# Rows of group means moved to the begin of the 1x1 stage, and SyncE's transfers there in another order

## The chip, the cores and the metric

The kernel runs on one core of one Trainium2 chip. The metric is the device time in microseconds (us) of one execution; lower is better. A core has five engines that work side by side, each through its own list of instructions, and that meet only at semaphores: TensorE (PE; its weight loads are shown as PEld), VectorE (DVE), ScalarE (ACT), GpSimd (POOL), and SyncE (SP), which here only issues DMA transfers.

## The reference, cut to what matters

```
x:   (32, 512, 48, 48) float32
# layer 0, h = group_norm(x, 32 groups)
f    = relu(Wc h + bc)                      # 1x1 convolution, 512 -> 128 channels
dynW = relu(f(mean of h, maxima of h))      # a 3x3 kernel for each image and channel pair
y    = conv3x3(f, dynW) + b_ad              # 128 -> 128 channels
x1   = x + Wf y + bf                        # 1x1 convolution, 128 -> 512 channels
# layer 1
out  = x1 + grouped conv3x3(group_norm(x1), kernels)   # 32 groups of 16 channels
```

## The kernel before, in words

The loop runs over the 32 images (n). The 512 channels are four chunks of 128 (Q = 4), the rows of an image five tiles (10, 10, 10, 10 and 8 rows of 48). TensorE works through four stages for an image, and each product is three matmuls (high by high, high by low, low by high; lines 853 to 855) on halves of a value that ScalarE and VectorE make:

- A, the first 1x1 convolution (`a_tile`): one bias matmul (line 862) and four chunks of three matmuls for each of five tiles. For each tile and chunk (i = 0 to 19) ScalarE makes the high half (`x_high`, line 442) and VectorE the low half (`x_low`, line 734), in a ring of five. So i = 0 to 4 can be made before the stage begins; they are, at the end of the image before (`X_LOW_AT`). After a tile ScalarE and VectorE take its result out of PSUM (`f_high`, `f_low`; line 743).
- B, the 3x3 convolution with the image's own kernels (`b_tile`): 27 matmuls for each of five tiles, with results taken out by `y_high` and `y_low` (line 751). Beside it VectorE takes moments and maxima (lines 604 and 612) of chunks 1, 2 and 3 of the next image.
- D and C interleaved: 16 pairs (r) of grouped convolutions of layer 1 for the image before (`d_pair`), and after pairs 0, 4, 8 and 11 the six units of one chunk of the second 1x1 convolution of this image (`c_unit`). VectorE adds the residuals (`output`, line 774; `residual`, line 764).

Layer 1 needs rows above and below the image: there the padding must be the group mean, so that it becomes zero once normalized. x1 goes to a scratch tensor in HBM (`write_x1`), and so do rows of means: VectorE writes `mrow`, 128 partitions x 4 chunks x 48 (`x1_group_means`, line 682), and SyncE sends it to the scratch tensor twice (`write_means`, lines 300 and 301). Then `load_t` (lines 319 to 321) brings x1 of image n-1 back, chunk by chunk, as bands of eight rows. `load_t` of chunk 0 waits for the landing of both transfers of means, and for the store of the last chunk of image n-2 out of the same slot (`stored`); chunks 1 and 2 follow on slots of their own.

The order of the work around the change is written out by hand. VectorE's list in `step(n)` is: for tiles 1 to 4 four (at tile 1, three) `x_low` and one `f_low`, a last `f_low`, then `x1_group_means(n-1)`, which begins with the rows of means, then `x1_variances(n-1)`, then B's work. The group means themselves are made by TensorE at the end of the step before (`x1_group_means` of TensorE, line 931, behind pair 15). SyncE's list in `step(n)` is: load chunk 1 of x for image n+1 (line 288), store the last chunk of image n-2 (line 326, which waits for VectorE's `output` of pair 15), load chunks 2 and 3 of x, write the means, load tiles 0, 1 and 2 of x1 of image n-1, then `write_x1(n, 0)` in the D and C stage. All of them go through one hardware queue.

Of the kernel before, what the change touches and what calls it, by code (L numbers as in the profile page):

```python
# [13 lines left out]
N, C, H, W = 32, 512, 48, 48  # L14
Q = C // P
# [66 lines left out]
def x_slot(c, odd):  # L82

    return c if c < 1 else c + 3 * odd


def partition_of(p):

    return GC * {0: 6, 7: 7}.get(p, p - 1)
# [7 lines left out]
def build(nc, x, wct, bc, kks_in, wrow_in, b_ad, wft, bf, kt, out):  # L97
# [7 lines left out]
    with ExitStack() as ctx:  # L105
# [142 lines left out]
        def t_slot(c):  # L248
            return tb[:, T_SLOT[c], :, :, :]
# [14 lines left out]
        def reached(eng, semaphore, value):  # L264

            if not isinstance(value, int) or value > 0:
                eng.wait_ge(semaphore, value)

        def images(eng, step):

            step(0, 0, d=False)
            step(1, 1)
            with nc.Fori(2, N - 2, 2, engines=[eng.engine], hint_back_edge=True) as n:
                step(n, 0)
                step(n + 1, 1)
            step(N - 2, 0)
            step(N - 1, 1, more=False)
# [4 lines left out]
        @block.sync  # L282
        def _(sp):
            def load_x(n, odd, c):

                if isinstance(n, int) and n == 1 and c in STATS_IN_B:
                    sp.wait_ge(max_done, Q)
                sp.dma_start(xb[:, x_slot(c, odd), :], x_d[n, c]).then_inc(x_in[c], 16)

            def write_x1(n, c):  # L290

                dst, made = sc_w[n, c, :, :, AT:AT + BW], n * CUNITS + (c + 1) * OR_
                sp.wait_ge(x1_done, made)
                sp.dma_start(dst, x1b[:, c % X1_SLOTS]).then_inc(x1_out[c], 16)

            def write_means(n):

                behind, ahead = sc_m[n, 0, :, :, AT + BW:AT + BW + W], sc_m[n, OR_ - 1, :, :, AT - W:AT]
                sp.wait_ge(mrow_done, n + 1)
                sp.dma_start(behind, mrow[:, :, :]).then_inc(behind_out, 16)  # L300
                sp.dma_start(ahead, mrow[:, :, :]).then_inc(ahead_out, 16)

            def load_t(n, c):

                written = (n + 1) * 16
                above, below = partition_of(0), partition_of(IR - 1)
                dst = t_slot(c).rearrange("p j b w -> p j (b w)")
                whole = sc_k[n, c, :, :, AT:AT + BW]
                over = sc_k[n, c, M6 - GC:M6, :, AT - W:AT - W + BW]
                under = sc_k[n, c, 0:GC, :, AT + W:AT + W + BW]  # L310
                sp.wait_ge(x1_out[c], written)
                if c == 0:
                    sp.wait_ge(behind_out, written)
                    sp.wait_ge(ahead_out, written)
                if T_SLOT[c] in T_SLOT[:c]:
                    sp.wait_ge(stored[T_SLOT.index(T_SLOT[c])], written)
                else:
                    sp.wait_ge(stored[Q - 1 if c == 0 else c], written)
                sp.dma_start(dst[0:M6], whole).then_inc(t_in[c], 16)
                sp.dma_start(dst[above:above + GC], over).then_inc(t_in[c], 16)  # L320
                sp.dma_start(dst[below:below + GC], under).then_inc(t_in[c], 16)

            def store(n, c):
                dst, made = out[n, c], n * PAIRS + (c + 1) * PER_CHUNK
                sp.wait_ge(out_done, made)
                sp.dma_start(dst, t_slot(c)[0:M6].rearrange("p j b w -> p (j b w)")).then_inc(stored[c], 16)

            def step(n, odd, d=True, more=True):
                if more:
                    load_x(n + 1, 1 - odd, 1)  # L330
                if not isinstance(n, int) or n >= 2:
                    store(n - 2, Q - 1)
                if more:
                    load_x(n + 1, 1 - odd, 2)
                    load_x(n + 1, 1 - odd, 3)
                if d:
                    if isinstance(n, int) and n == 1:
                        sp.wait_ge(k_lo, K_PARTS)
                    write_means(n - 1)
                    for c in range(Q - 1):  # L340
                        load_t(n - 1, c)
                write_x1(n, 0)
                if more:
                    load_x(n + 1, 1 - odd, 0)
                if d:
                    store(n - 1, 0)
                write_x1(n, 1)
                if d:
                    load_t(n - 1, Q - 1)
                    store(n - 1, 1)  # L350
                write_x1(n, 2)
                if d:
                    store(n - 1, 2)
                write_x1(n, 3)

            for c in range(Q):
                sp.dma_start(xb[:, x_slot(c, 0), :], x_d[0, c]).then_inc(x_in[c], 16)
            sp.wait_ge(vec_const, 1)
            for dst, src in ((wc[:, :, :], wct), (wf_once, wft), (wrow[0:GATES + 1, :], wrow_in), (kks[0:GATES, :], kks_in),
                             (gates[32:33, :], bc.rearrange("(a p) -> a p", a=1)),  # L360
                             (badc[:, :], b_ad.rearrange("(p a) -> p a", a=1)), (bfc[:, :], bf),
                             (bc_rows[0:1, 0, :], bc.rearrange("(a p) -> a p", a=1)),
                             (bc_rows[32:33, 0, :], bc.rearrange("(a p) -> a p", a=1)), (kt_once, kt_flat)):
                sp.dma_start(dst, src).then_inc(const_in, 16)

            sp.wait_ge(bands_zero, 1)
            for p in range(IR):
                lo, hi = max(0, p - 2), min(OR_ - 1, p)
                k, at = partition_of(p), 2 - p + lo
                sp.dma_start(stage[k:k + GC, :, lo * GC:(hi + 1) * GC],  # L370
                             kt[:, :, at * GC:(at + hi - lo + 1) * GC]).then_inc(kt_in, 16)
            images(sp, step)
            store(N - 2, Q - 1)
            write_means(N - 1)
            for c in range(Q - 1):
                load_t(N - 1, c)
            store(N - 1, 0)
            load_t(N - 1, Q - 1)
            for c in range(1, Q):
                store(N - 1, c)  # L380
            for c in range(Q):
                sp.wait_ge(stored[c], (N + 1 if c else N) * 16)
# [158 lines left out]
        def _(vec):  # L541
# [132 lines left out]
                vec.wait_ge(dve_stat, STAT_LINKS * n + 1)  # L674
                vec.tensor_scalar(nmean[:, :], vb[:, 0, :], -1.0 / PX, None, ALU.mult).then_inc(nmean_done, 1)

            def x1_group_means(n):

                vec.wait_ge(stat_mm2, 2 * n + 1)
                reached(vec, behind_out, n * 16)  # L680
                reached(vec, ahead_out, n * 16)
                vec.tensor_scalar(mrow[:, :, :], ps[:, 32:32 + Q].unsqueeze(2).to_broadcast([P, Q, W]), -1.0, None,
                                  ALU.mult).then_inc(mrow_done, 1)
                vec.tensor_tensor(vb[:, 1, :], ps[:, 32:32 + Q], nmean[:, :], ALU.subtract).then_inc(dve_stat, 1)
                vec.wait_ge(dve_stat, STAT_LINKS * n + 2)
                vec.tensor_tensor(vb[:, 2, :], vb[:, 1, :], vb[:, 1, :], ALU.mult).then_inc(dve_stat, 1)

                vec.wait_ge(cen_done, (n + 1) * Q)
                vec.tensor_tensor(vb[:, 3, :], cen[:, :], nmean[:, :], ALU.subtract).then_inc(dve_stat, 1)
                vec.wait_ge(dve_stat, STAT_LINKS * n + 4)  # L690
                vec.tensor_tensor(vb[:, 3, :], vb[:, 3, :], vb[:, 3, :], ALU.mult).then_inc(dve_stat, 1)
                vec.wait_ge(dve_stat, STAT_LINKS * n + 5)
                vec.tensor_tensor(vb[:, 2, :], vb[:, 2, :], vb[:, 3, :], ALU.subtract).then_inc(dve_stat, 1)
# [81 lines left out]
                                         op0=ALU.mult, op1=ALU.add).then_inc(out_done, 1)  # L775

            def step(n, odd, d=True, more=True):
                for t in range(NT):
                    for i in range(t * Q, (t + 1) * Q):
                        if i >= AHEAD:  # L780
                            x_low(n, odd, i)
                    if t:
                        f_low(n, t - 1)
                f_low(n, NT - 1)
                if d:
                    x1_group_means(n - 1)
                    x1_variances(n - 1)
# [9 lines left out]
                for r in range(PAIRS):  # L797
# [5 lines left out]
                    if more and r in MOMENTS_AT:  # L803
                        c, part = MOMENTS_AT[r]
# [33 lines left out]
                x_low(0, 0, i)  # L838
            dyn_low(0)
            images(vec, step)  # L840
            x1_group_means(N - 1)
            x1_variances(N - 1)
            for i in range(SCALE_STEPS):
# [183 lines left out]
```

## Time and profile before

| | us |
|---|---|
| median of 3 runs | 3616.2 (3615.72 to 3616.76) |
| the profiled execution | 3616.31 |
| span of the profiled execution, first to last instruction | 3614.6 |
| TensorE busy | 3498.8 (97%) |
| VectorE busy | 2532.3 (70%) |
| ScalarE busy | 2109.9 (58%) |
| GpSimd busy | 965.3 (27%) |
| mean granted TensorE clock | 0.992 |

The profile has a page (totals, the span in 40 slices, the chain of work that ended last, the costliest groups) and answers on a stretch of time: instructions in order of time, busy times of windows, who waited for whom, and DMA issues with the time from issue to landing. Times are from the span's start. A busy time of an engine is that of its instructions, and instructions of an engine overlap at their ends, so start-to-start distances tell more than durations.

### The profile page before, as it was taken

How to read it: one execution, taken by the hardware profiler on the slowest of the kernel's cores; microseconds unless marked ns; L12 is line 12 of the kernel's file. 1: busy time of each engine (PE TensorE's matmuls, PEld its weight loads, DVE VectorE, ACT ScalarE, POOL GpSimd, SP SyncE). 2: the span in 40 equal slices, each digit the busy share in tenths (PEclk: the TensorE clock that was granted, in tenths of full speed). 3: DMA queues.
4: the chain of work that ended last, by engine and by line, in shares of the span. 5: the costliest groups of instructions: out<-in, count | busy, mean ns of one | idle time of the engine just before them, and what ended most of it. 6: DMA issues, size and time to landing. Idle time of an engine off the chain costs nothing.

```text
span 3614.6 us, 60228 instructions
## 1 busy us (share of the span) xinstructions
PE 3498.8 (97%) x18688; PEld 2789.1 (77%) x18688; DVE 2532.3 (70%) x5365; ACT 2109.9 (58%) x3559; POOL 965.3 (27%) x1039
## 2 busy tenths in 40 slices
PE   5799999999999999999999999999999999999996
PEld 4677877777877778877778777778777778777785
DVE  7676777776767677777667777767777777776742
ACT  4365555665555665655655556655556655556654
POOL 2033222232222232222332222322222322223323
PEclk9899999999999999999999999999999999999998
DMA  5467767677767667767677667677676777676666
GB/s 122 142 193 190 190 178 185 200 195 192 185 180 195 191 184 193 190 183 197 189 188 190 186 178 207 197 190 186 178 191 194 188 195 186 182 199 187 170 156 158
DMA packets 317577, 666.88 MB, mean 184 GB/s; under 512 B 58863, under 2 KB 288242, under 8 KB 288645
## 3 DMA queue, kind: packets, MB, share of 16 engines
q1 hardware_dynamic: 317317, 663.34, 68.5%
q8 instruction: 172, 2.82, 0.3%
q14 instruction: 88, 0.72, 0.1%
HBM read 355.00 MB, written 308.28 MB: 184 GB/s over the span
## 4 chain that ended last, share of the span: by engine, by line
PE 90%; issue 5%; DVE 4%; DMA 1%; POOL 0%; DVEq 0%; ACT 0%; SPq 0%; POOLq 0%; ACTq 0%
PE pb L853 15%; PE pb L855 15%; PE pb L854 15%; PE pac L853 7%; PE pd L853 7%; PE pd L855 7%; PE pd L854 7%; PE pac L854 6%; PE pac L855 6%; PE pac L925 2%; PE pac L862 1%; DVE x1b L764 1%; PE ps L918 1%; DMA big<-x 0%; DVE va L596 0%
## 5 line engine op out<-in xcount | busy, mean ns | idle before, releaser
L407 POOL TENSOR_TENSOR hl<-un,hl 128x384 f16<-128x384 f32 x1024 | 937.6, 916 | 2570.2 <-ACT hl L432 2566.6
L432 ACT ACTIVATE hl<-un 128x384 f16<-128x384 f32 x1024 | 539.0, 526 | 427.8 <-PE pb L855 361.7
L428 ACT ACTIVATE un<-big,b_t,s_t 128x384 f32<-128x384 f32 x1024 | 709.7, 693 | 16.1 <-DMA big<-x_rows 16.1
L853 PE MATMUL pb<-fh,dynh 128*128 128x480 f32 (+1 forms) x1440 | 548.2, 381 | 0.0
L855 PE MATMUL pb<-fh,dynl 128*128 128x480 f32 (+1 forms) x1440 | 545.3, 379 | 0.0
L854 PE MATMUL pb<-fl,dynh 128*128 128x480 f32 (+1 forms) x1440 | 544.4, 378 | 0.0
L774 DVE SCALAR_TENSOR_TENSOR big<-pd,kout,big 96x768 f32<-96x768 f32 x256 | 258.8, 1011 | 382.6 <-PE pd L855 382.6
L853 PE MATMUL pd<-hl,k_h 128*96 128x384 f16 x1536 | 507.0, 330 | 18.8 <-POOL hl L407 18.8
L774 DVE SCALAR_TENSOR_TENSOR big<-pb,kout,big 96x768 f32<-96x768 f32 x256 | 258.9, 1011 | 351.8 <-PE pb L855 351.8
L853 PE MATMUL pb<-hl,k_h 128*96 128x384 f16 x1536 | 504.9, 329 | 0.0
L854 PE MATMUL pd<-hl,k_h 128*96 128x384 f16 x1536 | 504.8, 329 | 0.0
L855 PE MATMUL pd<-hl,k_l 128*96 128x384 f16 x1536 | 504.7, 329 | 0.0
L855 PE MATMUL pb<-hl,k_l 128*96 128x384 f16 x1536 | 504.0, 328 | 0.0
L854 PE MATMUL pb<-hl,k_h 128*96 128x384 f16 x1536 | 503.9, 328 | 0.0
L454 ACT ACTIVATE xs<-pb,badc 128x480 fp32r<-128x480 f32 (+1 forms) x160 | 103.3, 645 | 670.6 <-PE pb L855 670.6
L442 ACT ACTIVATE xs<-big,negm 128x480 fp32r<-128x480 f32 (+1 forms) x640 | 397.6, 671 | 80.9 <-PE pac L855 79.7
L734 DVE SCALAR_TENSOR_TENSOR xs<-big,negm,xs 128x480 fp32r<-128x480 f32 (+1 forms) x640 | 436.3, 733 | 9.5 <-ACT xs L442 9.4
L764 DVE SCALAR_TENSOR_TENSOR x1b<-pac,bfc,big 128x384 f32<-128x384 f32 x768 | 422.4, 607 | 6.2 <-PE pac L855 5.9
L604 DVE BATCH_NORM_STATS2 bst<-big 128x6 f32<-128x384 f32 x768 | 367.2, 543 | 9.4 <-DMA big<-x 9.3
L612 DVE TENSOR_REDUCE mx<-big 128x3 f32<-128x768 f32 x384 | 339.9, 939 | 0.0
L853 PE MATMUL pac<-xs,wfh 128*128 128x384 f32 x768 | 295.7, 385 | 35.5 <-DVE x1b L764 29.3
L855 PEld LDWEIGHTS pb<-fh,dynl 128*128 128x128 f32 x1440 | 270.8, 188 | 44.0
(115 smaller groups left out, 5241.6 us busy)
## 6 DMA issues: line engine op xcount, KB each, us to landing
big<-x SPq DMA_DIRECT2D x128, 1152.0 KB, 9.8
x_rows<-x1b SPq DMA_DIRECT2D x128, 1152.0 KB, 5.6
big<-x_rows SPq DMA_DIRECT2D x128, 1152.0 KB, 12.7
out<-big SPq DMA_DIRECT2D x128, 1152.0 KB, 6.2
big<-x_rows SPq DMA_DIRECT2D x256, 192.0 KB, 13.2
x_rows<-mrow SPq DMA_DIRECT2D x64, 96.0 KB, 1.9
big<-kt SPq DMA_DIRECT2D x4, 288.0 KB, 9.7
big<-kt SPq DMA_DIRECT2D x2, 192.0 KB, 11.0
```

The costliest lines, as they stand in the source:

```text
L407: pool.tensor_tensor(hl[:, g % HL_RING, 1, :, 1:W + 1], un[:, g % U_RING], hl[:, g % HL_RING, 0, :, 1:W + 1], ALU.subtract).then_inc(hl_lo, 1)
L428: act.activation(un[:, g % U_RING], t_slot(g // GQ)[:, g % GQ], ACT.Identity, bias=b_t[:, g:g + 1], scale=s_t[:, g:g + 1]).then_inc(u_done, 1)
L432: act.activation(hl[:, g % HL_RING, 0, :, 1:W + 1], un[:, g % U_RING], ACT.Copy).then_inc(hl_hi, 1)
L442: act.activation(xs_at(0, i, nr * W), xb[:, x_slot(c, odd), r0 * W:(r0 + nr) * W], ACT.Identity, bias=negm[:, c:c + 1]).then_inc(xs_hi, 1)
L604: ins = vec.bn_stats(bst[:, c, i, :], xb[:, x_slot(c, odd), i * HALF:(i + 1) * HALF])
L612: ins = vec.tensor_reduce(mx[:, c, 3 * band:3 * band + 3], src.rearrange("p (r l w) -> p l r w", r=CELL, l=3), AX.XY, ALU.max)
L734: vec.scalar_tensor_tensor(out=xs_at(1, i, nr * W), in0=xb[:, x_slot(c, odd), r0 * W:(r0 + nr) * W], scalar=negm[:, c:c + 1], in1=f32(xs_a ...
L764: vec.scalar_tensor_tensor(out=x1b[:, c % X1_SLOTS, k, :].rearrange("p (b w) -> p b w", w=W), in0=pac[:, u % C_BANKS, 0:BW].rearrange("p ( ...
L774: vec.scalar_tensor_tensor(out=dst, in0=pair_banks(p)[0:M6, :, 0:BW], scalar=kout[0:M6, 2:3], in1=dst, op0=ALU.mult, op1=ALU.add).then_inc ...
L853: pe.matmul(acc, high_w, high_x, start=start, stop=False)
L854: pe.matmul(acc, high_w, low_x, start=False, stop=False)
L855: return pe.matmul(acc, low_w, high_x, start=False, stop=stop)
```

## The change

VectorE: the rows of means, with their three waits, become `x1_mean_rows` and are issued at the very begin of `step(n)`, before the first `x_low` of the step (i = 5), instead of after the last `f_low`. The rest of `x1_group_means` stays where it was. SyncE: means and tile 0 are now issued before chunk 2 of x, and then tile 1, chunk 3 of x, tile 2. After the last image both lists have the same order as before.

```diff
                 if not isinstance(n, int) or n >= 2:
                     store(n - 2, Q - 1)
-                if more:
-                    load_x(n + 1, 1 - odd, 2)
-                    load_x(n + 1, 1 - odd, 3)
                 if d:
                     if isinstance(n, int) and n == 1:
                         sp.wait_ge(k_lo, K_PARTS)
                     write_means(n - 1)
-                    for c in range(Q - 1):
-                        load_t(n - 1, c)
+                    load_t(n - 1, 0)
+                if more:
+                    load_x(n + 1, 1 - odd, 2)
+                if d:
+                    load_t(n - 1, 1)
+                if more:
+                    load_x(n + 1, 1 - odd, 3)
+                if d:
+                    load_t(n - 1, 2)
                 write_x1(n, 0)
...
-            def x1_group_means(n):
+            def x1_mean_rows(n):
 
                 vec.wait_ge(stat_mm2, 2 * n + 1)
                 reached(vec, behind_out, n * 16)
                 reached(vec, ahead_out, n * 16)
                 vec.tensor_scalar(mrow[:, :, :], ps[:, 32:32 + Q].unsqueeze(2).to_broadcast([P, Q, W]), -1.0, None,
                                   ALU.mult).then_inc(mrow_done, 1)
+
+            def x1_group_means(n):
+
                 vec.tensor_tensor(vb[:, 1, :], ps[:, 32:32 + Q], nmean[:, :], ALU.subtract).then_inc(dve_stat, 1)
...
             def step(n, odd, d=True, more=True):
+                if d:
+                    x1_mean_rows(n - 1)
                 for t in range(NT):
                     for i in range(t * Q, (t + 1) * Q):
                         if i >= AHEAD:
...
             images(vec, step)
+            x1_mean_rows(N - 1)
             x1_group_means(N - 1)
```

## Rows read from the trace of the kernel before

**Rows 1.** The page, part 1: engine, busy us, share of the span, instructions.

```profile
PE 3498.8 (97%) x18688; PEld 2789.1 (77%) x18688; DVE 2532.3 (70%) x5365; ACT 2109.9 (58%) x3559; POOL 965.3 (27%) x1039
```

**Rows 2.** Windows of image 17, stages A and B: busy us by engine, clock, DMA share.

```profile
1897.65:1911.55 13.90, 13.90 (x68) 11.74 (x67) 13.78 (x23) 10.96 (x19) 0.00 (x0) 1.00 0.74 254
1911.55:1941.80 30.25, 30.25 (x143) 26.00 (x143) 21.81 (x47) 8.41 (x16) 3.58 (x4) 1.00 0.91 163
```

**Rows 3.** Timeline of VectorE, image 17, stage A: start, us, instruction, [idle before].

```profile
1898.50 1.00 DVE L774 SCALAR_TENSOR_TENSOR big<-pb,kout,big 96x768 f32<-96x768 f32 x1
1899.43 2.58 DVE L734 SCALAR_TENSOR_TENSOR xs<-big,negm,xs 128x480 fp32r<-128x480 f32 x4
1901.94 0.64 DVE L743 SCALAR_TENSOR_TENSOR fl<-pac,fh 128x480 fp32r<-128x480 f32 x1
...
1910.79 0.64 DVE L743 SCALAR_TENSOR_TENSOR fl<-pac,fh 128x480 fp32r<-128x480 f32 x1
1912.28 0.56 DVE L743 SCALAR_TENSOR_TENSOR fl<-pac,fh 128x384 fp32r<-128x384 f32 x1 [0.84 <-ACT fh L448]
1912.75 0.35 DVE L682 TENSOR_SCALAR mrow<-ps 128x192 f32<-128x192 f32 x1
1913.02 0.15 DVE L684 TENSOR_TENSOR vb<-ps,nmean 128x4 f32<-128x4 f32 x1
```

**Rows 4.** Timeline of TensorE, image 17, first matmuls of the last tile of A.

```profile
1909.33 0.44 PE L853 MATMUL pac<-xs,wch 128*128 128x384 f32 x1
1909.61 0.33 PE L854 MATMUL pac<-xs,wch 128*128 128x384 f32 x1
```

**Rows 5.** Timeline of VectorE, `x_low` 0 and 1 of image 2 and of image 17.

```profile
249.75 2.31 DVE L734 SCALAR_TENSOR_TENSOR xs<-big,negm,xs 128x480 fp32r<-128x480 f32 x2
...
1892.72 2.41 DVE L734 SCALAR_TENSOR_TENSOR xs<-big,negm,xs 128x480 fp32r<-128x480 f32 x2
```

**Rows 6.** Timeline of TensorE, first matmul of A and of B, images 2 and 17.

```profile
254.68 0.47 PE L862 MATMUL pac<-onesr,bmat 128*128 128x480 f32 x1
...
268.49 0.39 PE L853 MATMUL pb<-fh,dynh 128*128 128x480 f32 x1
...
1897.65 0.46 PE L862 MATMUL pac<-onesr,bmat 128*128 128x480 f32 x1
...
1911.55 0.39 PE L853 MATMUL pb<-fh,dynh 128*128 128x480 f32 x1
```

**Rows 7.** Timelines of VectorE and TensorE, image 1, last tile of A.

```profile
155.32 2.20 DVE L734 SCALAR_TENSOR_TENSOR xs<-big,negm,xs 128x384 fp32r<-128x384 f32 x4
...
156.57 0.34 PE L853 MATMUL pac<-xs,wch 128*128 128x384 f32 x1
156.75 0.34 PE L854 MATMUL pac<-xs,wch 128*128 128x384 f32 x1
```

**Rows 8.** Timeline of SyncE's queue, image 17: the store, and the first transfer of tile 2.

```profile
1899.66 0.33 SPq L326 DMA_DIRECT2D out<-big  x1
...
1920.59 0.58 SPq L319 DMA_DIRECT2D big<-x_rows  x1
```

**Rows 9.** DMA issues there: KB each, us to landing (store, x chunk 3, tiles 0 and 2, means).

```profile
out<-big SPq DMA_DIRECT2D x1, 1152.0 KB, 6.2
...
big<-x SPq DMA_DIRECT2D x1, 1152.0 KB, 11.9
...
big<-x_rows SPq DMA_DIRECT2D x1, 1152.0 KB, 8.7
...
big<-x_rows SPq DMA_DIRECT2D x1, 1152.0 KB, 20.5
...
x_rows<-mrow SPq DMA_DIRECT2D x1, 96.0 KB, 1.9
```

**Rows 10.** Timeline of VectorE, image 17, stage B: moments of chunk 3, and the last `y_low`.

```profile
1932.93 2.84 DVE L604 BATCH_NORM_STATS2 bst<-big 128x6 f32<-128x384 f32 x6
...
1941.83 0.62 DVE L751 SCALAR_TENSOR_TENSOR xs<-pb,badc,xs 128x384 fp32r<-128x384 f32 x1 [2.85 <-ACT xs L454]
```

## The prediction

> **What bounds the kernel now.** I read the page first. TensorE is busy for 97% of the span, every other engine for 70% or less [rows 1], so a change elsewhere counts only where it makes TensorE wait. Then I asked for windows of one image in the middle of the span. In stage A (13.90 us) VectorE is busy 13.78 us of 13.90, more than its 70% by far; in stage B it has 21.81 of 30.25 [rows 2]. TensorE reads 13.90 of 13.90, but a busy matmul in this view may be one that is stretched, so that row can't show small waits.
>
> The timeline decides who leads in A. VectorE's row of instructions runs from `output` of pair 15 at 1898.50 to the `f_low` of 1910.79 with no idle time before any of them; only the last `f_low`, at 1912.28, has waited, 0.84 us, for ScalarE [rows 3]. On the other side TensorE's first two matmuls of the last tile are 1909.61 - 1909.33 = 0.28 us apart [rows 4], where the same two in image 1 are 156.75 - 156.57 = 0.18 apart [rows 7]: TensorE waited 0.1 us there for a low half. So in image 17 VectorE sets the pace of A's end, by a small margin, and TensorE has no slack left to give.
>
> The trace holds its own experiment on that. `x_low` 0 and 1 take 2.31 us together in image 2 and 2.41 in image 17 [rows 5], so VectorE comes 0.10 us earlier into A in image 2. A lasts 268.49 - 254.68 = 13.81 us in image 2 and 1911.55 - 1897.65 = 13.90 in image 17 [rows 6]. A tenth of a microsecond on VectorE's list is a tenth on TensorE's: one to one. Read image by image, images 2 to 31, 30 of them, have one of these two lengths within 0.02 us.
>
> **The change part by part.** *The rows of means on VectorE.* One instruction moves from behind the last `f_low` to between `x_low` 4 and `x_low` 5. Behind it in its new place stand the other 15 `x_low` and five `f_low` of the stage, and TensorE waits for each of these `x_low`. Its duration is 0.35 us, but the next instruction starts 1913.02 - 1912.75 = 0.27 us after it [rows 3], because neighbours overlap at their ends; the gap, 0.27 (0.264 before rounding), is what it costs in a row of instructions with no idle time. Its three waits are met in the new place: the group means' matmul stands behind pair 15 and in front of A's first matmul, at 1897.65 [rows 6], and VectorE gets there after `x_low` 4, at about 1899.43 + 2.58 / 4 = 1900.1 [rows 3]; the means of the image before were sent 109 us earlier. Nobody waits here for long. The waits are taken in by the sequencer while `x_low` 4 runs, as they now are while the last `f_low` runs: from that `f_low` to the means is 1912.75 - 1912.28 = 0.47 us for an instruction of 0.56 [rows 3], so they add nothing visible.
>
> What it takes away behind the last `f_low` is worth nothing: there VectorE had just been idle for 0.84 us [rows 3] and what follows is needed only after B's first tile.
>
> So each A stage in which VectorE leads grows by 0.264 us: 30 images (2 to 31) x 0.264 = 7.9 us. In image 0 there are no rows of means. In image 1 the last tile's `x_low` begins at 155.32 and, at 2.20 / 4 = 0.55 us each, ends at about 155.9, 0.7 us before TensorE takes it at 156.57 [rows 7]; 0.26 us fits in there, so image 1 costs nothing. After image 31 the order is the old one: nothing.
>
> Bounds of this term: not below 0 if all of it fell into slack, which rows 3, 4 and 6 speak against; and not above the full duration of 0.35 us if nothing overlapped: 30 x 0.35 = 10.5 us. I take 0.264, the row measured in this very instruction.
>
> The Trainium skill (VectorE: DVE Perf Modes, section on the TRN2 errata) gives 120 cycles plus one per element at 0.96 GHz for a VectorE instruction that reads PSUM: by that, 192 elements would be an estimated (120 + 192) / 0.96 = 325 ns, and the sum 30 x 0.325 = 9.8 us. The trace has 0.35 us for the duration and 0.27 from start to start [rows 3]; the second is what a full list pays, so the measurement decides.
>
> *SyncE's list.* The means can go out at about 1900.1 + 0.35 = 1900.5 instead of 1913.26. But tile 0 must also wait for the store that SyncE issued at 1899.66 and that lands 6.2 us later, at 1905.9 [rows 8, 9]. The means, whose own landing takes 1.9 us [rows 9], now share the queue with that store; I put the landing of both at about 1907.5. SyncE stands in that wait, and chunks 2 and 3 of x and tiles 1 and 2 are queued behind it. Before, the chunks of x went out at 1900.
>
> Now the landings, taking the queue as one row of work. Tiles 0 to 2 together: tile 0 needs 8.7 us from its issue, and tile 2, issued at 1920.59, lands 20.5 us later at 1941.1 [rows 8, 9]; three of them take about 25 us, 8.2 each. The store and two chunks of x together, 1899.66 to 1900.7 + 11.9 = 1912.6, take 13 us, of which the two chunks are 1912.6 - 1905.9 = 6.7, or 3.4 each. New order: tile 0 at 1907.5 + 8.7 = 1916.2, chunk 2 at 1919.6, tile 1 at 1927.8, chunk 3 at 1931.2, tile 2 at 1939.4. VectorE begins on chunk 3 at 1932.93 [rows 10], and with the 0.26 us of above at 1933.2: chunk 3 is there 2 us ahead. Chunk 2 is wanted some 6 us before chunk 3 and comes 12 us before it. The tiles of x1 come no later than now. If chunk 3 were late, VectorE still has 2.85 us of idle time before the last `y_low` [rows 10], so up to about 2 + 2.85 = 4.8 us of error in my landings cost nothing. Price of SyncE's part: 0. Its gain: 0 too, since no engine waits for x1's tiles or for chunks 2 and 3 in the middle of the span; earlier landings only lengthen a lead.
>
> **Sum.** Against the profiled execution: 3614.6 + 7.9 = 3622.5 for the span, and with the 1.7 us around it (3616.31 - 3614.6) 3624.2. That execution lies 0.1 us from the median of the runs, 3616.2; so the predicted median is 3624.1, slower by 0.22%.
>
> **The rivals.**
> - *The instruction is absorbed; no change.* It would hold if VectorE had a lead on TensorE at A's end. For it: in image 1 the lead is 0.7 us [rows 7], and in rows 3 VectorE has time just after A. Against it: rows 4 and 6. Price 0 to 4 us, time 3616 to 3620. Chance 0.10.
> - *A transfer is late.* The means' small packets and the store share the queue, tile 0 holds up SyncE, and chunk 3 of x comes after the 1936.0 (1933.2 + 2.85) from which it costs. If it landed only with tile 2, at 1939.4, the last `y_low` would be 1939.4 - 1936.0 = 3.4 us late; x 30 images = some 100 us, on top of the 7.9: 3725. For it: SyncE now stands 5 us or more in a wait in front of x's chunks. Against it: in the rows of now the landings come in the order of the issues [rows 8, 9]. Chance 0.06.
> - *Not slower but faster: the transfers are spread.* The DMA share is 0.74 in A and 0.91 in B [rows 2]. If loads into SBUF slowed the instructions beside them, the 8.2 us of tile 0's load that leave B would give time back in B, on the engine that leads there, TensorE. It decides once it gives back more than 0.264 us an image, so once a load slows its neighbours by 0.264 / 8.2 = 3%; at 8% it gives 0.66 us, net 0.4 us x 30 = 12 us: 3604. For it: TensorE leads in B without a pause [rows 2]. Against it: what leaves B enters A, where VectorE leads and would be slowed in turn, and no row shows an instruction stretched beside a load. Chance 0.04.
> - *More than the row:* the sequencer is late for the short instruction and the one behind it, up to 0.35 us or somewhat more; 10.5 to 14 us, 3627 to 3630. Chance 0.08.
>
> **How the numbers follow.** The forecast has what is left, 0.72. The range for 8 in 10 reaches from 3618 (part of the first rival) to 3631 (the fourth): it leaves out most of the first, the second and the third rival, under 0.2. About 0.2%, 7.2 us, is what a measurement of this kernel tells from no change, and my 7.9 stands just above: within the forecast I give 0.15 to a measured difference under 7.2. So slower by over 0.2%: 0.72 x 0.85 + 0.06 + 0.08 = 0.75. Within 0.2%: 0.72 x 0.15 + 0.10 = 0.21. Faster: 0.04.
>
> **What would show it.** In the changed profile: the distance from A's first to B's first matmul 14.16 us instead of 13.90 in image 17, and 14.07 in image 2; image 1 unchanged; VectorE without idle time from pair 15's `output` to the second last `f_low`, with `mrow` in front of the second `x_low`; the idle time before the last `f_low` still about 0.84. The first transfer of tile 0 issued at about 10 us after A's begin, and none of VectorE's moments waiting for a DMA in the middle of the span. If A is still 13.90, the first step is wrong; if A is 14.16 and the time is not 8 us longer, another stage gave time back; if moments wait for x, the landings were.

## The result, and the profile after

| | before | after |
|---|---|---|
| median of 20 runs each, us | 3615.36 (3612.03 to 3616.9) | 3623.15 (3620.86 to 3625.0) |
| ratio, 95% interval | | 1.0021 (1.0014 to 1.0028) |
| span of the profiled execution, us | 3614.6 | 3619.6 |

The change costs 7.8 us, slower by 0.21%; 7.9 was forecast. The interval reaches from 5 to 10 us, so the agreement to a tenth is luck, and the profile's rows below are the sharper test. The answers of the profile after stand in the order of the rows of before. First the windows view of image 17, stage A (busy us of TensorE, its weight loads, VectorE, ScalarE, GpSimd, then the granted clock, the DMA share and GB/s), beside [rows 2]:

```profile
1898.61:1912.77 14.16, 14.16 (x68) 11.58 (x67) 14.04 (x24) 11.13 (x19) 0.00 (x0) 1.00 0.62 156
```

Stage A lasts 14.16 us where it was 13.90. VectorE's timeline there, beside [rows 3]:

```profile
1900.38 0.70 DVE L741 SCALAR_TENSOR_TENSOR xs<-big,negm,xs 128x480 fp32r<-128x480 f32 x1
1901.01 0.34 DVE L686 TENSOR_SCALAR mrow<-ps 128x192 f32<-128x192 f32 x1
1901.28 1.96 DVE L741 SCALAR_TENSOR_TENSOR xs<-big,negm,xs 128x480 fp32r<-128x480 f32 x3
...
1912.01 0.64 DVE L750 SCALAR_TENSOR_TENSOR fl<-pac,fh 128x480 fp32r<-128x480 f32 x1
1913.49 0.56 DVE L750 SCALAR_TENSOR_TENSOR fl<-pac,fh 128x384 fp32r<-128x384 f32 x1 [0.84 <-ACT fh L452]
```

`mrow` takes 1901.28 - 1901.01 = 0.27 us from start to start in its new place too, no instruction up to the second last `f_low` has waited, and the idle time before the last `f_low` is the same 0.84 us. TensorE's timeline, first matmul of A and of B in image 2, then of A in image 31, beside [rows 6]:

```profile
251.74 0.46 PE L872 MATMUL pac<-onesr,bmat 128*128 128x480 f32 x1
...
265.81 0.39 PE L863 MATMUL pb<-fh,dynh 128*128 128x480 f32 x1
...
3435.77 0.46 PE L872 MATMUL pac<-onesr,bmat 128*128 128x480 f32 x1
```

Image 2's A is 265.81 - 251.74 = 14.07 us, 0.26 more than its 13.81 of before. From A of image 2 to A of image 31 it is 3184.03 us; before it was 3431.22 - 254.68 = 3176.54. The difference is 7.49 us over 29 images, 0.26 each.

The two profiled spans differ by 5.0 us only, because these two executions differ in their first 250 us, where the clock falls at another moment each time. The windows view of 100 to 160 us, before and then after (the clock is the third number from the end):

```profile
100.00:160.00 60.00, 37.64 (x140) 31.06 (x139) 37.65 (x93) 26.09 (x40) 0.00 (x0) 0.72 0.43 158
```

```profile
100.00:160.00 60.00, 37.60 (x160) 31.08 (x160) 38.55 (x103) 26.24 (x41) 0.00 (x0) 0.80 0.59 176
```

At a mean granted clock of 0.80 instead of 0.72 TensorE does 160 matmuls there instead of 140, and image 2 begins 254.68 - 251.74 = 2.9 us earlier. Where the clock falls there differs from execution to execution; the medians are what count.

SyncE's queue and landings, image 17, beside [rows 8, 9]: issue times, and KB with us to landing for chunk 2 of x, chunk 3 of x and the main part of tile 2.

```profile
1907.60 0.62 SPq L319 DMA_DIRECT2D big<-x_rows  x1
...
1909.87 0.50 SPq L288 DMA_DIRECT2D big<-x  x1
...
1912.97 4.60 SPq L288 DMA_DIRECT2D big<-x  x1
1917.74 0.69 SPq L319 DMA_DIRECT2D big<-x_rows  x1
```

```profile
big<-x SPq DMA_DIRECT2D x1, 1152.0 KB, 14.0
...
big<-x SPq DMA_DIRECT2D x1, 1152.0 KB, 22.9
...
big<-x_rows SPq DMA_DIRECT2D x1, 1152.0 KB, 20.5
```

Chunk 2 lands at 1923.9, chunk 3 at 1935.9. VectorE's timeline in B shows what that does, beside [rows 10]:

```profile
1935.85 2.86 DVE L608 BATCH_NORM_STATS2 bst<-big 128x6 f32<-128x384 f32 x6 [1.60 <-DMA big<-x]
...
1943.06 0.62 DVE L758 SCALAR_TENSOR_TENSOR xs<-pb,badc,xs 128x384 fp32r<-128x384 f32 x1 [1.15 <-ACT xs L458]
```

VectorE now waits 1.60 us for chunk 3, and its idle time before the last `y_low` has shrunk from 2.85 to 1.15 us. Image 17 is one of the milder ones: of images 2 to 30 all but image 11 have such a wait, 0.3 to 4.0 us long, and chunk 3 lands between A + 35.7 and A + 39.6, A + 37.5 in the mean. The longest wait is in image 15, whose A begins at 1679.04; VectorE's timeline there, then TensorE's first matmul that takes the last `y_low`:

```profile
1718.62 2.86 DVE L608 BATCH_NORM_STATS2 bst<-big 128x6 f32<-128x384 f32 x6 [3.96 <-DMA big<-x]
1721.40 2.65 DVE L616 TENSOR_REDUCE mx<-big 128x3 f32<-128x768 f32 x3
1723.97 1.23 DVE L758 SCALAR_TENSOR_TENSOR xs<-pb,badc,xs 128x480 fp32r<-128x480 f32 x2
...
1725.49 0.48 PE L863 MATMUL pac<-xs,wfh 128*128 128x384 f32 x1
```

No idle time is left before the last `y_low` there. It is done at 1723.97 + 1.23 = 1725.20, 0.3 us before TensorE takes it; in image 17, where it is done at 1943.68 and taken at 1945.07, that second margin is 1.4 us, as in the kernel before. So the wait costs nothing yet in any image, but in one the cover over it is nearly gone.

### The profile page after: what moved, and what is told of

It is laid out like the page before. It is cut to its first block, busy times and chain, and to the rows that moved or that the text cites. A ratio compares the mean times of both kernels' runs of the same rounds, so it can differ in the third digit from the quotient of the medians.

```text
span 3619.6 us, 60228 instructions
## 1 busy us (share of the span) xinstructions
PE 3503.9 (97%) x18688; PEld 2781.6 (77%) x18688; DVE 2534.1 (70%) x5365; ACT 2114.4 (58%) x3559; POOL 965.2 (27%) x1039
## 4 chain that ended last, share of the span: by engine, by line
PE 90%; issue 5%; DVE 4%; DMA 1%; POOL 0%; DVEq 0%; ACT 0%; SPq 0%; POOLq 0%; ACTq 0%
PE pb L863 15%; PE pb L865 15%; PE pb L864 15%; PE pac L863 7%; PE pd L863 7%; PE pd L865 7%; PE pd L864 7%; PE pac L864 6%; PE pac L865 6%; PE pac L935 2%; DVE x1b L771 1%; PE pac L872 1%; PE ps L928 1%; DMA big<-x 0%; DVE va L600 0%
```

## The experiments

Runs on one chip shared their runs of the kernel before (medians 3615.9, 3615.8 and 3615.7).

**VectorE's part alone.** SyncE's list is the old one; the rest as changed. The difference from the kernel before, in words:

```diff
-                    the rows of means first in x1_group_means(n - 1)
+                    x1_mean_rows(n - 1) at the begin of step(n)
```

> Only VectorE's part of the change: the rows of means at the begin of stage A, SyncE's list as before. My theory: the whole cost is that one instruction in front of fifteen low halves, 0.264 us in each of 30 images. Stage A of image 17 lasts 14.16 us (before 13.90, after 14.16), the time is 7.9 us above before and equal to after (about 3623 where before is 3615.4), and no moments wait for x in the middle of the span (after: 65.3 us in 30 waits). Rival, the new order of transfers carries half or more of the cost: the time is within 4 us of before.

Measured: 3621.6 us, ratio 1.0019 (1.0010 to 1.0028). TensorE's A of image 17 runs from 1898.42 to 1912.59, 14.17 us. VectorE's waits for a chunk of x are 9.5 us in 2 waits, both in the first 203 us. From A of image 3 on each image takes 109.8 us, as in the changed kernel, and 109.5 in the kernel before. So the whole slowdown is here (5.7 us in the medians, 3.6 to 10.1 by the interval), and the wait for chunk 3 belongs to the other part.

**SyncE's part alone.** The rows of means stay behind the last `f_low`. SyncE's list, in words:

```diff
-                    load x 2, load x 3, means, tile 0, tile 1, tile 2
+                    means, tile 0, load x 2, tile 1, load x 3, tile 2
```

> Only SyncE's part: new order of transfers, the rows of means where they were, behind the last low half of the 3x3 stage's input, so SyncE sends them 13 us later and chunks 2 and 3 of x wait behind them. In the changed kernel chunk 3 lands 28.3 us after the issue of tile 0; tile 0 would now be issued 18.3 us after A's begin, so chunk 3 lands at A + 46.6 where VectorE wants it at A + 35.3 and has 2.85 us to spare. With 5.5 us of moments and maxima and two low halves behind it, the last low half of B comes at about A + 53.5, and TensorE, which wants it at about A + 46.5, waits 7 us an image: 30 x 7 = 210 us, a range of 3770 to 3860. Rival, the transfers' order never matters because x is loaded an image ahead: 3615.

Measured: 3790.2 us, ratio 1.0480 (1.0464 to 1.0496), in the range. VectorE's timeline of image 17, whose A begins at 1990.13:

```profile
2035.47 2.86 DVE L608 BATCH_NORM_STATS2 bst<-big 128x6 f32<-128x384 f32 x6 [6.47 <-DMA big<-x]
2038.24 2.66 DVE L616 TENSOR_REDUCE mx<-big 128x3 f32<-128x768 f32 x3
2040.81 1.24 DVE L755 SCALAR_TENSOR_TENSOR xs<-pb,badc,xs 128x480 fp32r<-128x480 f32 x2
```

Chunk 3 lands at A + 45.3 (46.6 was expected), the last two `y_low` end at A + 51.9, and TensorE waits for them. That the time is in the range is partly luck: TensorE's waits for `y_low` are 111.8 + 8.5 us, 4.0 an image instead of the 7 expected, and the lower clock behind them, which wasn't forecast, makes up part of the rest (see the last experiment). So the two halves of the change belong together: the list alone costs 174 us, the rows alone the few us of the changed kernel, and the early rows are what makes the new list harmless.

**Rows in front of the last tile.** SyncE's list as before.

```diff
                 for t in range(NT):
+                    if t == NT - 1 and d:
+                        x1_mean_rows(n - 1)
                     for i in range(t * Q, (t + 1) * Q):
```

> SyncE's list as before; the rows of means in front of the last tile's four low halves (i = 16 to 19) instead of in front of i = 5. My theory, VectorE's list is full from pair 15 on and all that counts is that the instruction stands before the last low half: the same 7.9 us as at the begin, stage A 14.16 us. Rival, what costs is the lead lost at the begin, and it can be made up between: less, 0 to 4 us, and a stage A under 14.05 us.

Measured: 3623.4 us, 1.0021 (1.0012 to 1.0030); A is 1915.35 - 1901.18 = 14.17 us. The price is the same behind eleven `x_low` more, so it isn't a lost lead that could be made up: the list is full all the way.

**An instruction of the same shape more.** It writes to a place that isn't read.

```diff
+                reached(vec, hl_lo, n * G)
+                vec.tensor_scalar(un[:, 0, 0:Q, :], ps[...], -1.0, None, ALU.mult)
                 vec.tensor_scalar(mrow[:, :, :], ps[...], -1.0, None, ...)
```

> As the changed kernel, with a second instruction of the same shape (its result goes to a place that is not read) in front of the rows of means. My theory: another 0.26 to 0.27 us in each of 30 images: stage A of image 17 14.43 us, the time 8 us above the changed kernel, 15.8 above before (about 3631). Rival by the duration and not by the distance of starts, 0.35 us: 10.4 us above the changed kernel, 3634. Rival, the first 0.26 us was a step that happens once (a wait that VectorE now just misses): equal to the changed kernel, 3623.

Measured: 3630.7 us, 1.0040 (1.0026 to 1.0054), 14.8 above before; A is 1920.11 - 1905.67 = 14.44 us. Twice the instruction, twice the cost: 0.54 us above the 13.90 of before. The distance of starts (0.27) prices it, the duration (0.35) is too much.

This run also tells about image 1, since the granted clock in that image's A happens to be the same as in the profile before. Windows of A of image 1, before and then here:

```profile
142.21:158.67 16.46, 16.46 (x66) 14.34 (x66) 13.44 (x22) 13.78 (x23) 0.00 (x0) 0.81 0.36 153
142.19:158.58 16.39, 16.39 (x66) 14.31 (x67) 13.95 (x24) 13.78 (x23) 0.00 (x0) 0.82 0.72 146
```

With two instructions more in VectorE's list A isn't longer there, where it is 0.54 us longer in image 17.

**Rows made by ScalarE.** It has idle time at the begin of A.

```diff
+            def mean_rows(n):                        # ScalarE, at the begin of step(n)
...
+                act.activation(mrow[:, :, :], ps[:, 32:32 + Q]..., ACT.Copy, scale=-1.0)
```

> As the changed kernel, but ScalarE makes the rows of means, at the begin of its stage A, where it has 2.5 us of idle time; VectorE waits for them only behind its last f_low. My theory: the cost was VectorE's list alone, so stage A of image 17 is 13.90 us again and the time that of before, about 3615.5, though the transfers stay in the new order and moments still wait 1.6 us for chunk 3. Rival, the early means and tile loads cost TensorE something by themselves: 3619 to 3623.

Measured: 3620.4 us, 1.0011 (1.0002 to 1.0020), 4.6 us above before, where no loss was expected. A is 1911.06 - 1897.17 = 13.89 us, as expected, and images 3 to 29 take 109.50 to 109.54 us each; before they took 109.52 to 109.57. The loss sits in image 30 alone, the first behind the loop, which takes 114.8. VectorE's timeline there:

```profile
3336.68 0.16 DVE L704 TENSOR_TENSOR vb<-vb 128x4 f32<-128x4 f32 x1
3344.11 0.16 DVE L710 SCALAR_TENSOR_TENSOR vb<-m,vb 128x4 f32<-128x4 f32 x1 [7.27 <-issue]
```

and TensorE's, which waits for the result behind B's first tile:

```profile
3340.68 0.38 PE L866 MATMUL pb<-fh,dynl 128*128 128x480 f32 x1
3344.65 0.43 PE L947 MATMUL ps<-spread,ones 128*128 128x64 f32 x2 [3.59 <-DVE spread L715]
3344.90 0.70 PE L864 MATMUL pb<-fh,dynh 128*128 128x480 f32 x1
3345.40 0.60 PE L865 MATMUL pb<-fl,dynh 128*128 128x480 f32 x1
3345.80 0.60 PE L866 MATMUL pb<-fh,dynl 128*128 128x480 f32 x1
```

"issue" means that VectorE waited for nothing that the profile shows: 7.27 us, where the kernel before has a gap of 2.1 us nearby. TensorE loses 3.6 us, and after the pause its matmuls are 0.40 us apart instead of 0.23 for about 3.4 us: the granted clock is at the lower of its two levels, which costs 1.7 us more. Together that is the 5.3 us of image 30.

**ScalarE's rows with SyncE's old list, early and late.** Two runs to find where the gap comes from; VectorE's list is the same in all three. In the second of them ScalarE makes the rows behind its last `f_high`. SyncE's list against the ScalarE version above, in words:

```diff
-                    means, tile 0, load x 2, tile 1, load x 3, tile 2
+                    load x 2, load x 3, means, tile 0, tile 1, tile 2
```

> ScalarE makes the rows at the begin of A, as in the run before with ScalarE, but SyncE's list is the old one (chunks 2 and 3 of x, then means, then tiles 0 to 2). Open question: the 4.6 us that ScalarE's version lost came in one image only, number 30, the first behind the loop, where VectorE stood still for 7.3 us (2.1 before) at A + 15.8 with nothing to wait for but its instructions. Theory 1, the fetch of its instructions stands behind the transfers that are in the queue at that moment: here the tiles still go out early, behind x, so the queue is full at A + 15.8, the gap is again 5 us or more and the time about 3620. Theory 2, the new order of the list makes it: gap 2.1, 3615.5.

> As the run above, but ScalarE makes the rows at the end of A, behind its last f_high, so means and tiles go out at about A + 15 as in the kernel before; VectorE's list is instruction for instruction that of the other two ScalarE versions. Theory 1 (fetch behind queued transfers): at A + 15.8 the queue is nearly empty, the gap in image 30 is about 2 us, hidden in VectorE's idle time, and the time is that of before, 3615.5. Rival, the place of the block of instructions that is fetched in VectorE's shorter list makes the gap: 7.3 us again, about 3620.

Measured: 3615.3 us, 0.9998 (0.9989 to 1.0007), and 3615.6, 1.0000 (0.9991 to 1.0009). The gaps are 1.8 and 1.95 us, in the second:

```profile
3338.72 0.16 DVE L706 SCALAR_TENSOR_TENSOR vb<-m,vb 128x4 f32<-128x4 f32 x1 [1.95 <-issue]
```

The expectation for the first was wrong, but in its premise: I took the tiles to go out early there. They don't; the means stand behind x's two chunks, and tile 0 is issued at 3337.81, A + 16.3. The DMA view of 3334 to 3340 us (for each kind of queue packets, MB and share of the 16 engines; "instruction" is code) shows what was in the queue. The ScalarE version with the new list:

```profile
q1 hardware_dynamic: 654, 1.08, 113.1%
```

and with the old list and late rows:

```profile
q1 hardware_dynamic: 1074, 0.29, 19.8%
q8 instruction: 1, 0.02, 1.2%
q14 instruction: 2, 0.02, 1.0%
```

In the first, data has all of the engines (113%) and not one packet of code moves in these 6 us; in the second three packets of code do. So with VectorE's list unchanged, the gap is 7.3 us where the tiles are in flight when code is wanted and 2 us where they aren't. In the first the next packets of code move only between 3340 and 3344 us, and the changed kernel, which has no gap in image 30, has two small ones early, in 3333 to 3336 us (A + 7 to A + 10), when the data packets have stopped and those of tile 0 haven't begun. The two views:

```profile
q1 hardware_dynamic: 345, 1.33, 96.2%
q8 instruction: 1, 0.02, 1.6%
q14 instruction: 1, 0.01, 0.5%
```

```profile
q1 hardware_dynamic: 616, 0.11, 19.9%
q14 instruction: 2, 0.02, 1.4%
```

In all seven profiles with this gap (before, SyncE's part alone, `dyn_low` earlier on the kernel before, and the four with ScalarE's rows) a packet of 8 KB on q14 ends 1.2 to 1.7 us before the gap does, so it may be the one that VectorE waits for. That it waits behind the data is the reading that fits these runs; it isn't shown, since the profile says neither when a packet of code was asked for nor whose it is. Nor is it shown why the changed kernel's packets move so much earlier. A full queue at A + 16 alone doesn't make the gap: the changed kernel has that too.

**dyn_low one pair earlier, on both kernels and on ScalarE's.**

```diff
-DYN_LOW_AT = 13
+DYN_LOW_AT = 12
```

> The kernel before with one instruction of VectorE, dyn_low (1.27 us from start to start), behind pair 12's output instead of pair 13's; there VectorE is idle for 3.9 us. Output of pair 15 can then start when TensorE is done with the pair, 0.75 us earlier (A + 0.10 instead of A + 0.85), and VectorE has a lead at A's end. My theory: TensorE's waits in A go, 13.64 instead of 13.90 us in 28 images and 0.16 us less in two: 7.6 us, about 3608. Rival, TensorE's waits in A have another cause (stretched matmuls): 3615.5 and stage A 13.90.

> The changed kernel with the same move of dyn_low. Of the 0.75 us that it frees, 0.26 go for the waits of before and 0.26 for the rows of means; 0.23 are left. My theory: the rows of means now cost nothing: stage A 13.64 us, the time that of the kernel before with the same move, about 3608, so the change is 0 here and 7.9 there. Rival, an added instruction costs its length wherever it stands in A: 3616.

> ScalarE makes the rows at the begin of A, new order of transfers, and dyn_low behind pair 12. Stage A 13.63 us in all 30 images, as with VectorE's rows and the same move of dyn_low (3607.4), so no gain from ScalarE there; and the gap of VectorE in image 30 stays, since list and queue at that moment are the same: 4 to 5 us more, about 3612. Rival: with 0.5 us more lead the gap is hidden, 3607.5.

Measured: on the kernel before 3609.0 us, 0.9981 (0.9972 to 0.9990); on the changed kernel 3607.4, 0.9976 (0.9966 to 0.9986); on ScalarE's version 3612.9, 0.9992 (0.9983 to 1.0001). A is 1907.20 - 1893.56 = 13.64 us in the first and 1906.81 - 1893.17 = 13.64 in the second. VectorE's timeline of the second:

```profile
1885.37 1.36 DVE L670 SCALAR_TENSOR_TENSOR dynl<-pac,dynh 128x1152 fp32r<-128x1152 f32 x1 [1.99 <-ACT dynh L489]
...
1893.24 1.01 DVE L781 SCALAR_TENSOR_TENSOR big<-pb,kout,big 96x768 f32<-96x768 f32 x1 [0.40 <-PE pb L865]
1894.17 0.70 DVE L741 SCALAR_TENSOR_TENSOR xs<-big,negm,xs 128x480 fp32r<-128x480 f32 x1
1894.80 0.35 DVE L686 TENSOR_SCALAR mrow<-ps 128x192 f32<-128x192 f32 x1
1895.06 1.37 DVE L741 SCALAR_TENSOR_TENSOR xs<-big,negm,xs 128x480 fp32r<-128x480 f32 x2
```

`output` of pair 15 now waits for TensorE, at A + 0.07 instead of A + 0.85, and the rows of means, still 0.26 us long, cost nothing. The same instruction in the same place is worth 7.8 us or 0, by the lead of its engine. Both versions beat both kernels; their intervals overlap. The third keeps the gap of image 30 (6.7 us), as expected, and is 5.6 us slower than with VectorE's rows; in its profile image 30 lasts 112.6 instead of 109.3 us, and this time the clock doesn't fall. The other 2 us of the difference aren't placed.

**Chunk 3 last.** The changed kernel with tile 2 in front of chunk 3.

```diff
-                    tile 0, load x 2, tile 1, load x 3, tile 2
+                    tile 0, load x 2, tile 1, tile 2, load x 3
```

> The changed kernel with chunk 3 of x issued behind tile 2 instead of in front of it. In the changed kernel tile 2 lands 5.6 us after chunk 3, so chunk 3 now lands at about A + 42.9. With 5.4 us of moments and maxima and two low halves of 0.6 us the last low half is done at A + 49.6, where TensorE wants it at A + 46.45: 3.1 us in each of 30 images, 94 us above the changed kernel, about 3717, range 3680 to 3740. Rival, queue position within these few us doesn't matter: 3623.

Measured: 3775.8 us, 1.0435 (1.0419 to 1.0451); expected were 3680 to 3740. VectorE's timeline of image 17 (A begins at 1983.66), then windows of the same image:

```profile
2026.61 2.86 DVE L607 BATCH_NORM_STATS2 bst<-big 128x6 f32<-128x384 f32 x6 [7.32 <-DMA big<-x]
2029.38 2.65 DVE L615 TENSOR_REDUCE mx<-big 128x3 f32<-128x768 f32 x3
2031.96 1.23 DVE L757 SCALAR_TENSOR_TENSOR xs<-pb,badc,xs 128x480 fp32r<-128x480 f32 x2
```

```profile
2020.00:2033.00 13.00, 10.42 (x57) 8.93 (x55) 6.39 (x11) 6.33 (x11) 4.15 (x5) 1.00 0.34 99
2033.20:2036.60 3.40, 3.36 (x11) 3.36 (x12) 2.23 (x6) 0.00 (x0) 0.00 (x0) 0.52 0.00 0
```

The chain was right to a tenth: landing at A + 42.95 (42.9), last `y_low` done at A + 49.5 (49.6), TensorE's waits 106.2 us in 30 waits, 3.5 each (3.1). What the sum lacked is the clock: behind the pause of image 17 it is 0.52 for 3.4 us. Other images fare otherwise. Windows behind the pause of image 16, and of image 8:

```profile
1918.20:1923.80 5.60, 5.60 (x18) 5.60 (x19) 3.76 (x10) 0.00 (x0) 0.00 (x0) 0.50 0.00 0
...
997.20:1005.00 7.80, 7.80 (x46) 6.62 (x47) 5.14 (x14) 2.76 (x4) 0.89 (x1) 1.00 0.33 116
```

Images 2 to 30 of this profile, counted by how long the clock stays at the lower level, against the 109.8 us of the changed kernel:

| stretch at the lower level | images | TensorE's wait for `y_low`, us | longer than the changed kernel, us |
|---|---|---|---|
| none | 2 | 3.1 | 3.1 |
| 3.4 us | 11 | 3.4 | 4.8 |
| 6.8 us, in part inside the wait | 16 | 3.8 | 6.2 |

In the mean a wait of 3.6 us made an image 5.45 us longer, half as much again as the wait. The median of the runs is 153 us above the changed kernel, 153 / 30 = 5.1 an image. The same surcharge is in the profile of SyncE's part alone (mean clock 0.975 against 0.992).

## Why the prediction was right, step by step

- *VectorE sets the pace of A's end, and a tenth there is a tenth on TensorE.* Shown: 0.26 us at the begin, 0.27 in front of the last tile, 0.54 for two instructions, 0 where VectorE has a lead.
- *The cost is the distance of starts, 0.264 us, in 30 images.* Shown: A 14.16 in image 17 and 14.07 in image 2, both as forecast; doubled by a second instruction. The price by the duration that the Trainium skill's formula gives (VectorE: DVE Perf Modes, section on the TRN2 errata), an estimated 9.8 us, would have been 2 us off; a list that is full pays 0.27 for this shape.
- *Image 1 costs nothing.* The profile after can't tell: its A was 15.1 us instead of 16.5, by the clock, which hides 0.26. The run with two instructions does: 16.39 against 16.46 us at a like clock.
- *SyncE's part costs 0.* The price was right, by its margin; a step below it failed: "chunk 3 is there 2 us ahead" and that no moments would wait. Chunk 3 landed at A + 37.26 where A + 33.55 was forecast, 3.7 us later, 1.6 behind VectorE's want; 4.8 us of error was what the text allowed. In image 15 it was A + 39.6, 6 us later than forecast and beyond that allowance. It cost nothing even so, because the last `y_low` is done 1.4 us before TensorE takes it, a margin that the forecast left out; 0.3 us of it remained. I had taken the queue as one row of work. Tile 0 came as reckoned (A + 17.4, forecast A + 18.6), but chunk 2 came 7.9 us after it instead of 3.4. Its last pieces moved beside tile 1's, not in front of them: for 1920.6 to 1923.9 us, the last before it landed, the DMA view counts 459 packets under 2 KB, the size of a tile's, and 3 over 8 KB, the size of a chunk's. The main part of tile 2 landed at A + 39.6 (forecast A + 41.7), its last part at A + 42.9, so the batch as a whole was not late. Order of issue still gave the order of landing in image 17, but not its times. The Trainium skill (DMA: Bandwidth & Descriptors, section on two DMAs through the same engine) says that nothing orders transfers across the 16 engines; no landing out of order in these rows shows that.
- *The rivals.* Absorbed: excluded in this kernel, and real with `dyn_low` earlier. A late transfer: real, and in image 15 only 0.3 us away. Its condition was put 1.4 us too early by the margin left out, and its price, 100 us for 3.4 us an image, too low by half, since each wait also costs clock. Gain by spreading: nothing, since ScalarE's rows with either list take the same 109.5 us an image. More than the row: excluded, at 0.27 us an instruction.

## What to carry to other kernels

Before an instruction is moved, look whether its engine has idle time between that place and the next point where the leading engine waits for it; a list without idle time prices every insertion at its start-to-start distance times the iterations, whatever the engine's share of the span says. The mean share of VectorE was 70%, in this stage it was 99%. And when a transfer is moved up in a queue, reckon the batch as a whole and give single landings several us of play (here 3.9 us between images of one execution). What is still hidden afterwards is worth reading in every image: in image 17 the idle time fell from 2.85 to 1.15 us, in image 15 to nothing, with no sign of it in the time.

## What the runs showed of the hardware

- After pauses of TensorE of 2.0 to 5.4 us behind B the granted clock was at the lower of its two levels for 3.4 us in 11 of 29 images and for 6.8 us in 16, and such images lost 1.4 and 2.4 us more than the pause; after pauses of 3.0 and 3.2 us in the other two it didn't fall (chunk 3 last). So the length of the pause alone didn't decide here.
- Code is moved by the same 16 DMA engines as data (q8 and q14 beside q1). Behind the loop VectorE stood still for 1.8 to 2.2 us in five profiles with a queue that wasn't full then, and for 6.7 and 7.3 us in two where tile loads filled it; the changed kernel, whose two 8 KB packets of code had moved before the tile loads, had no such gap. That the code waited behind the data fits, and isn't shown.
- Chunks of x queued between tile loads landed, in one execution, at moments 3.9 us apart from image to image (chunk 3: A + 35.7 to A + 39.6).
